# Two layers on one core: an iteration loop written out, row maxima turned by TensorE and sent in two transfers, expert products in new places of the engines' orders

## Chip, core and metric

One core of a Trainium2 chip runs the whole kernel. The metric is the device time of one execution in microseconds (us).

## What is computed

The input x has 2 sequences of 4096 tokens with 512 channels (float32). Two layers follow, cut here to what matters:

```python
# layer 1, "mix": an RWKV recurrence over the tokens, per channel
h = layernorm(x); k = h @ Wk.T; r = h @ Wr.T; v = r
y = wkv_scan(-exp(time_decay), time_first, k, v)   # stable, with a running maximum
x = x + (sigmoid(r) * y) @ Wo.T
# layer 2, "att" and "moe"
h = rmsnorm(layernorm(x)); q = h @ Wq + bq; kv = (h @ Wdown + bdown) @ Wup + bup
att = softmax(q k / sqrt(32))       # over the 16 heads of ONE token, no mixing of tokens
x2 = layernorm(x) + (att @ v) @ Wo + bo
gate = softmax(rmsnorm(x2) @ Wg + bg)             # 8 experts, all of them used
out = x + x2 + sum_e gate_e * (rmsnorm(x2) @ We[e])
```

## The kernel before

The 8192 tokens are cut into 32 tiles of 256. A software pipeline of 34 iterations works on three tiles at once: iteration i does the recurrence ("mix") of tile i, the attention ("att") of tile i-1, the experts ("moe") of tile i-2, and the first norm ("pre") of tile i+1. Each engine walks through its own hand-written list of steps, the same in every iteration (`PE_ORDER`, L132; `DVE_ORDER`, L142; `ACT_ORDER`, L154; `POOL_ORDER`, L164; `SP_ORDER`, L169), and waits on semaphores where it needs another engine's result. An engine never overtakes in its own list, so a step that waits holds up all that stands behind it. `pipeline` (L336) issues the iterations: 0 to 3 written out, 4 to 29 as a hardware loop of 13 passes with two iterations in each (`Fori`, L364), 30 to 33 written out again. In iterations 0 and 1 the expert slots split the weights instead.

Products in float16 have three passes of high and low halves. One expert product, ("moe", u), is one expert for 128 tokens: 12 matmuls of 128x512 into one of two banks (`moe`, L1253); VectorE multiplies it by its gate and adds it to `acc` (`moe`, L1052, the instruction at L1060). There are 16 of them per tile. TensorE may start product u when VectorE is done with u-2.

The attention of one tile, in the order of the data:

- `att_q` (TensorE L1180, ScalarE L630 by way of `heads`, L633) and `att_up` (L1187, L647) make q, k and v. SyncE's `att_up` (L429) copies them by 16 transfers into the stacks `qs` and `ks` (L438 and L442); VectorE's `att_stack` (L975) copies the other rows of `ks`.
- `att_max` (TensorE L1204, the matmuls at L1213): 8 groups of raw scores, "M" 0 to 7, each 4 matmuls into one of a ring of four banks; a group may start when the maximum of the group four before it is done. VectorE takes the maximum of each row (L991) into `mcol` (128 x 32). ("att_max", n) stands for groups 2n and 2n+1.
- `att_m`: VectorE turns `mcol` within squares of 32 (L996) and splits it into two float16 rows (L998, L1000); SyncE sends them into two rows of `qs` with 8 transfers (L445 to L449), so that the next products subtract the maxima by themselves.
- `att_scores` (TensorE L1217, matmuls at L1222; ScalarE's exponential L657) and `att_probs` (TensorE L1226, matmuls at L1232; VectorE divides, L1002): 8 groups each, S0 to S7 and P0 to P7, in the same ring of four banks. P is in float32: for each group 8 recorded matmuls with only 33 columns and 128x128 weights. P k waits for exponential k, and for VectorE's division of P k-2.
- `att_back`, `att_project`, `att_turn2`, `att_gate` end the attention.

In the recurrence, for each half of the channels: VectorE's `mix_decay` (L878), ScalarE's `mix_exp` (L579: four Relu and three exponentials), VectorE's `mix_sum`, `mix_value`, `mix_scan`, `mix_rec` and `mix_gate`, with ScalarE's `mix_num` (L593), and `mix_split` at the end. `mix_project` (TensorE, line names `bank<-w_o,xo`) is the last product that a recurrence tile needs; its start is the mark by which iterations are measured here.

Of the kernel before, what the change touches and what calls it, by code (L numbers as in the profile page):

```python
# [115 lines left out]
ATT_BANK = {use: n % ATT_RING for n, use in enumerate(ATT_USES)}  # L116


def att_before(use):
# [25 lines left out]
    ("mix_value", 0), ("moe", 4), ("att_max", 0), ("att_max", 1), ("att_max", 2), ("att_max", 3), ("att_m", 0),
    ("moe", 5), ("mix_scan", 0), ("moe", 6), ("mix_rec", 0), ("moe", 7), ("mix_rec", 1), ("mix_gate", 0), ("moe", 8),
    ("mix_split", 0), ("att_probs", 0), ("att_probs", 1), ("moe", 9), ("att_probs", 2), ("att_probs", 3),
    ("mix_decay", 1), ("att_probs", 4), ("att_probs", 5), ("moe", 10), ("att_probs", 6), ("att_probs", 7),
    ("att_back", 0), ("mix_sum", 1), ("mix_value", 1), ("moe", 11), ("moe", 12), ("mix_scan", 1), ("att_project", 0),
# [5 lines left out]
    ("mix_turn", 0), ("att_norm", 0), ("moe_gate", 0), ("att_turn", 0), ("mix_k", 0), ("moe", 0), ("moe", 1),  # L155
    ("att_latent", 0), ("att_q", 0), ("att_up", 0), ("mix_v", 0), ("moe", 2), ("moe", 3), ("mix_exp", 0), ("moe", 4),
    ("moe", 5), ("moe", 6), ("moe", 7), ("mix_num", 0), ("att_rest", 0), ("att_scores", 0), ("moe", 8), ("moe", 9),
    ("att_scores", 1), ("mix_split", 0), ("att_scores", 2), ("att_scores", 3), ("att_scores", 4), ("att_scores", 5),
# [15 lines left out]
def build(nc, x, wk, wr, wo1, decay, first, gamma1, wq, bq, wdown, bdown, wup, bup, wo2, bo, gamma2,  # L174
          wg, bg, we, ident_in, kmask_in, qmask_in, out):
    with ExitStack() as ctx:
# [1129 lines left out]
```

## Time and profile before

| | us |
|---|---|
| median of 3 runs | 3222.83 |
| lowest, highest | 3214.9, 3233.78 |
| the profiled execution | 3235.43 |
| its span, first to last instruction | 3233.6 |
| TensorE busy in the span | 2904.1 (90%) |
| VectorE, ScalarE, GpSimd busy | 2221.2 (69%), 1286.2 (40%), 619.2 (19%) |
| mean granted TensorE clock | 0.933 of full speed |

The profile names TensorE PE (PEld: its weight loads), VectorE DVE, ScalarE ACT, GpSimd POOL, SyncE SP; SPq is SyncE's transfer queue. A timeline row has start, length, engine, line, operation, output<-inputs, shapes and a count of merged instructions; in brackets the idle time before it and what ended it. A row of windows has one stretch, its length, the busy time of each engine (with instructions), then the granted clock (1.00 is 2.4 GHz, 0.50 is 1.2 GHz, the only two levels; a value between them is a mix over the stretch), the share of the transfer engines and GB/s.

### The profile page before, as it was taken

The numbers are of one execution on the slowest core, as the hardware profiler recorded it, in microseconds if no ns is written. First come the engines' busy times: TensorE is split into PE (matmuls) and PEld (weight loads), VectorE is DVE, ScalarE is ACT, GpSimd is POOL, SyncE is SP. The second block draws the span as 40 slices with busy tenths as digits, with TensorE's granted clock in tenths as the row PEclk, the third lists the DMA queues.
The fourth block names the chain that finished last, engine by engine and source line by source line (L and its number), as shares of the span: only waits on it lengthen the run. The fifth ranks groups of instructions, "written<-read, shape, count | busy, mean of one in ns | idle before, by whom it ended". The sixth has DMA issues, their size and how long they took to land.

```text
span 3233.6 us, 53881 instructions
## 1 busy us (share of the span) xinstructions
PE 2904.1 (90%) x18864; PEld 1822.3 (56%) x18864; DVE 2221.2 (69%) x4132; ACT 1286.2 (40%) x2399; POOL 619.2 (19%) x681
## 2 busy tenths in 40 slices
PE   2359999999999999999999999999999899999989
PEld 2236665655665655656565565556566565566644
DVE  4787777677666767767676766767766666776663
ACT  2354443433443434444343444444344343444421
POOL 0111122211212212112221121222111221212120
PEclk9669999898999989999998999999899999999999
DMA  6011221101121201121210111220112120212110
GB/s 198 16 18 27 34 34 27 31 24 28 27 34 28 34 21 27 27 34 27 34 31 24 27 27 28 34 34 23 26 27 34 28 33 21 34 21 34 27 20 14
DMA packets 588333, 102.96 MB, mean 32 GB/s; under 512 B 556562, under 2 KB 556690, under 8 KB 588050
## 3 DMA queue, kind: packets, MB, share of 16 engines
q1 hardware_dynamic: 588068, 99.40, 18.0%
q8 instruction: 170, 2.79, 0.4%
q14 instruction: 95, 0.78, 0.1%
HBM read 48.49 MB, written 16.78 MB: 20 GB/s over the span
## 4 chain that ended last, share of the span: by engine, by line
issue 63%; POOL 13%; PE 11%; DVE 7%; SPq 3%; ACT 2%; DMA 1%; POOLq 1%; DVEq 0%; ACTq 0%
PE bank L1080 8%; POOL k L498 2%; POOL x L493 2%; POOL qo L498 2%; POOL acc L520 2%; PE bank L1232 2%; POOL ev L484 2%; POOL zz L480 1%; DVE wkv L895 1%; SPq L442 1%; SPq L438 1%; DVE w_e L827 1%; DVE zz L919 1%; DVE mcol L991 1%; POOL rs L511 1%
## 5 line engine op out<-in xcount | busy, mean ns | idle before, releaser
L1080 PE MATMUL bank<-w_e,h2t 128*128 128x512 f16 x6144 | 1459.4, 396 | 25.8 <-DVE acc L1060 25.8
L1080 PEld LDWEIGHTS bank<-w_e,h2t 128*128 128x128 f16 x6144 | 617.8, 102 | 771.8 <-issue 109.6
L1060 DVE SCALAR_TENSOR_TENSOR acc<-bank,gates,acc 128x512 f32<-128x512 f32 x512 | 370.1, 733 | 173.8 <-PE bank L1080 173.8
L595 ACT ACTIVATE e<-v 128x512 f32<-128x512 f32 x64 | 40.5, 633 | 737.1 <-DVE wkv L895 737.1
L480 POOL TENSOR_TENSOR zz<-wkv,zz 128x512 f32<-128x512 f32 x64 | 105.3, 1645 | 1112.8 <-DVE ev L906 1112.8
L1232 PEld LDWEIGHTS bank<-vp,pr 128*128 128x128 f32 x2048 | 286.6, 214 | 12.8 <-issue 2.4
L1232 PE MATMUL bank<-vp,pr 128*128 128x33 f32 x2048 | 290.8, 292 | 1.9 <-ACT pr L661 1.9
L661 ACT ACTIVATE pr<-bank,col 128x512 f32<-128x512 f32 x256 | 172.5, 686 | 249.1 <-PE bank L1222 249.1
L1080 PE MATMUL bank<-w_o,xo 128*128 128x512 f16 x768 | 176.0, 387 | 78.9 <-DVE xo L857 78.9
L991 DVE TENSOR_REDUCE mcol<-bank 128x4 f32<-128x512 f32 x256 | 158.8, 682 | 114.2 <-PE bank L1213 114.2
L895 DVE TENSOR_TENSOR_SCAN wkv<-e,wkv 128x256 f32<-128x256 f32 x256 | 233.9, 955 | 2.0 <-ACT e L590 2.0
L980 DVE COPY ks<-k 32x1024 f16<-32x1024 f16 x256 | 120.7, 472 | 158.5 <-ACT k L644 151.5
L919 DVE RECIPROCAL zz<-zz 128x256 f32<-128x256 f32 x128 | 223.0, 1743 | 0.0
L498 POOL TENSOR_TENSOR qo<-t,qo 128x256 f16<-128x256 f32 x128 | 87.8, 686 | 467.0 <-ACT qo L644 467.0
L1080 PE MATMUL bank<-w_o,qo 128*128 128x512 f16 x768 | 172.7, 382 | 4.1 <-DVE qo L857 4.1
L1080 PE MATMUL bank<-xo,w_k 128*128 128x256 f16 x1536 | 174.6, 274 | 0.0
L1080 PE MATMUL bank<-ht,w_q 128*128 128x256 f16 x1536 | 173.4, 273 | 0.0
L1080 PE MATMUL bank<-xo,w_r 128*128 128x256 f16 x1536 | 172.9, 273 | 0.0
L1080 PEld LDWEIGHTS bank<-w_o,xo 128*128 128x128 f16 x768 | 73.7, 99 | 173.2 <-DVE xo L857 60.8
L1080 PEld LDWEIGHTS bank<-xo,w_k 128*128 128x128 f16 x1536 | 151.3, 98 | 17.9
L1080 PEld LDWEIGHTS bank<-ht,w_q 128*128 128x128 f16 x1536 | 150.6, 98 | 17.7
L1080 PEld LDWEIGHTS bank<-xo,w_r 128*128 128x128 f16 x1536 | 150.3, 98 | 17.4
(177 smaller groups left out, 3678.7 us busy)
## 6 DMA issues: line engine op xcount, KB each, us to landing
qs<-qo SPq DMA_DIRECT2D x384, 64.0 KB, 3.4
xk<-in_attn_x SPq DMA_DIRECT2D x32, 512.0 KB, 3.6
x<-in_attn_x SPq DMA_DIRECT2D x32, 512.0 KB, 3.6
result<-acc SPq DMA_DIRECT2D x32, 512.0 KB, 2.8
ks<-k SPq DMA_DIRECT2D x128, 64.0 KB, 3.3
w_e<-in_ffn_We SPq DMA_DIRECT2D x7, 1024.0 KB, 13.5
qs<-m SPq DMA_DIRECT2D x256, 2.0 KB, 1.7
qs<-in_attn_Wk SPq DMA_DIRECT2D x1, 1024.0 KB, 5.5
```

Source lines behind the costliest of these rows:

```text
L480: nc.gpsimd.tensor_tensor(zz[:, :, :], wkv[:, 2, :, 0:T], zz[:, :, :], ALU.add).then_inc(mix_pool.sem, 1)
L484: nc.gpsimd.tensor_tensor(ev[:, :, :], wkv[:, 1, :, 0:T], ev[:, :, :], ALU.add).then_inc(mix_pool.sem, 1)
L493: nc.gpsimd.tensor_tensor(x2[:, s, :], x2[:, s, :], bo_row[:, :], ALU.add).then_inc(att_pool.sem, 1)
L498: nc.gpsimd.tensor_tensor(grouped(dst, 1)[:, :, b, :], t32[:, b % 2, :].rearrange("p (g j) -> p g j", g=G), grouped(dst, 0)[:, :, b, :], A ...
L661: nc.scalar.activation(pr[:, k % 2, :], att_bank[ATT_BANK["S", k]][:, :], ACT.Exp, scale=colof["soft"])\
L895: V.tensor_tensor_scan(wkv[:, n, c, 1:T + 1], e1[:, c, :], src[:, c, :], wkv[:, n, c, 0:1], ALU.mult, ALU.add).then_inc(mix_dve.sem, 1)
L919: V.reciprocal(zz[:, c, :], zz[:, c, :]).then_inc(mix_dve.sem, 1)
L980: V.tensor_copy(ks[n * HD:(n + 1) * HD, :, f, :], grouped(k16, 0)[f * HD:(f + 1) * HD].rearrange("p g b j -> p g (b j)")).then_inc(att_dve ...
L991: V.tensor_reduce(mcol[:, 4 * k:4 * k + 4], att_bank[ATT_BANK["M", k]][:, :].rearrange("p (g x) -> p g x", g=4), AX, ALU.max).then_inc(att ...
L1060: V.scalar_tensor_tensor(out=acc[:, s, :], in0=moe_bank[u % 2][:, :], scalar=gates[:, s, e:e + 1], in1=acc[:, s, :], op0=ALU.mult, op1=ALU ...
L1080: ins = nc.tensor.matmul(dst, left(a), right(b), start=(n == 0), stop=(n == last))
L1232: ins = nc.tensor.matmul(att_bank[ATT_BANK["PV", k]][:, n * (HD + 1):(n + 1) * (HD + 1)], pr[:, k % 2, n * P:(n + 1) * P], vp[:, 4 * k + n ...
```

## The change

- `pipeline` issues all 34 iterations written out; the hardware loop is gone.
- Row maxima: TensorE turns `mcol` (new step ("att_m", 0) of `PE_ORDER`, a transposition 128x32 into 32 partitions x 128 of the bank of M7), VectorE splits it from there (two instructions in place of three), and SyncE sends each of the two rows with one transfer, 2 in place of 8. The ring's wait for the bank of M7 is moved to the split.
- New orders for TensorE, VectorE and ScalarE. On TensorE, among the steps around the attention: expert product 2 goes ahead of `att_up`; 3, 4 and 5 stand before the maxima, which are then in one piece; 6, the turn, 7 and 8 follow; 9 stays after S0 and S1; 10 and 11 go in among the score and value products, 12 and 13 between them and `att_project`. On VectorE, 0 and 1 go ahead of `att_latent` and 2 ahead of `mix_decay`; `att_vt` is ahead of 3; the second half's `mix_decay`, `mix_sum` and `mix_value` go in among the divisions. On ScalarE, the second `mix_exp` goes between exponentials 4 and 5, and `mix_num` 0 behind exponential 1.

```diff
 PE_ORDER = [
     ("mix_turn", 0), ("moe", 0), ("moe", 1), ("att_turn", 0), ("mix_k", 0), ("att_latent", 0), ("att_q", 0),
-    ("att_up", 0), ("mix_v", 0), ("moe", 2), ("moe", 3), ("moe", 4), ("att_max", 0), ("att_max", 1), ("moe", 5),
-    ("att_max", 2), ("att_max", 3), ("moe", 6), ("moe", 7), ("moe", 8), ("att_scores", 0), ("att_scores", 1),
-    ("moe", 9), ("att_probs", 0), ("att_scores", 2), ("att_probs", 1), ("att_scores", 3), ("att_probs", 2),
-    ("att_scores", 4), ("att_probs", 3), ("att_scores", 5), ("att_probs", 4), ("att_scores", 6), ("att_probs", 5),
-    ("att_scores", 7), ("moe", 10), ("att_probs", 6), ("att_probs", 7), ("moe", 11), ("moe", 12), ("att_project", 0),
-    ("moe", 13), ("moe", 14), ("moe", 15), ("att_turn2", 0), ("mix_project", 0), ("att_gate", 0),
+    ("moe", 2), ("att_up", 0), ("mix_v", 0), ("moe", 3), ("moe", 4), ("moe", 5), ("att_max", 0), ("att_max", 1),
+    ("att_max", 2), ("att_max", 3), ("moe", 6), ("att_m", 0), ("moe", 7), ("moe", 8), ("att_scores", 0),
+    ("att_scores", 1), ("moe", 9), ("att_probs", 0), ("att_scores", 2), ("att_probs", 1), ("att_scores", 3),
+    ("att_probs", 2), ("att_scores", 4), ("moe", 10), ("att_probs", 3), ("att_scores", 5), ("att_probs", 4),
+    ("moe", 11), ("att_scores", 6), ("att_probs", 5), ("att_scores", 7), ("att_probs", 6), ("att_probs", 7),
+    ("moe", 12), ("moe", 13), ("att_project", 0), ("moe", 14), ("moe", 15), ("att_turn2", 0), ("mix_project", 0),
+    ("att_gate", 0),
 ]
 DVE_ORDER = [
...
+    ("att_stats", 0), ("att_norm", 0), ("mix_turn", 0), ("moe_gate", 0), ("att_turn", 0), ("moe", 0), ("moe", 1),
+    ("att_latent", 0), ("moe", 2), ("mix_decay", 0), ("att_stack", 0), ("att_vt", 0), ("moe", 3), ("mix_sum", 0),
+    ("moe", 4), ("mix_value", 0), ("att_max", 0), ("att_max", 1), ("att_max", 2), ("att_max", 3), ("moe", 5),
+    ("att_m", 0), ("moe", 6), ("mix_scan", 0), ("mix_rec", 0), ("moe", 7), ("mix_rec", 1), ("mix_gate", 0),
+    ("moe", 8), ("att_probs", 0), ("mix_split", 0), ("att_probs", 1), ("mix_decay", 1), ("att_probs", 2), ("moe", 9),
+    ("att_probs", 3), ("att_probs", 4), ("mix_sum", 1), ("mix_value", 1), ("moe", 10), ("att_probs", 5), ("moe", 11),
+    ("att_probs", 6), ("att_probs", 7), ("att_back", 0), ("mix_scan", 1), ("mix_rec", 2), ("moe", 12), ("moe", 13),
+    ("att_project", 0), ("mix_rec", 3), ("mix_gate", 1), ("moe", 14), ("mix_split", 1), ("pre_stats", 0), ("moe", 15),
...
 ACT_ORDER = [
...
+    ("moe", 5), ("moe", 6), ("moe", 7), ("att_rest", 0), ("att_scores", 0), ("att_scores", 1), ("moe", 8),
+    ("mix_num", 0), ("mix_split", 0), ("moe", 9), ("att_scores", 2), ("att_scores", 3), ("att_scores", 4),
+    ("mix_exp", 1), ("att_scores", 5), ("moe", 10), ("att_scores", 6), ("att_scores", 7), ("moe", 11),
...
-        m_in = Steps(sem("m_in"), 16, m=2 * F)
+        m_in = Steps(sem("m_in"), 16, m=2)
...
-                    "M": (att_dve, "smax", k), "S": (att_act, "ex", k), "PV": (att_dve, "norm", 2 * k + 1),
+                    "M": (att_dve, "m_lo", 0) if k == 7 else (att_dve, "smax", k), "S": (att_act, "ex", k), "PV": (att_dve, "norm", 2 * k + 1),
...
-            for i in range(4):
-                iteration(i, i % 2, i // 2)
-            with eng.Fori(0, (NT - 6) // 2) as pair:
-                for par in range(2):
-                    iteration(pair * 2 + (4 + par), par, pair + 2)
-            for i in range(NT - 2, NT + 2):
+            for i in range(NT + 2):
                 iteration(i, i % 2, i // 2)
...
-                    for f in range(F):
-                        sp.dma_start(qs[SCAN_ROWS + l:SCAN_ROWS + l + 1, :, f, :], m16[f * G:(f + 1) * G, l, :]).then_inc(m_in.sem, 16)
+                    sp.dma_start(qs[SCAN_ROWS + l:SCAN_ROWS + l + 1, :, :, :].rearrange("a g f x -> a g (f x)"), m16[:, l, :]).then_inc(m_in.sem, 16)
...
-                dve.wait_ge(*att_dve.done(t, "smax"))
-                V.transpose(mturn[:, :], mcol[:, :]).then_inc(att_dve.sem, 1)
-                dve.wait_ge(*att_dve.done(t, "m_turn"))
-                V.tensor_scalar(m16[:, 0, :], mturn[:, :], -2.0 ** -14, None, ALU.mult).then_inc(att_dve.sem, 1)
+                turned_m = att_bank[TURNED_M][0:G, 0:P]
+                dve.wait_ge(*att_pe.done(t, "MT0"))
+                V.tensor_scalar(m16[:, 0, :], turned_m, -2.0 ** -14, None, ALU.mult).then_inc(att_dve.sem, 1)
...
+            def att_m(t, _):
+                pe.wait_ge(*att_dve.done(t, "smax"))
+                nc.tensor.transpose(att_bank[TURNED_M][0:G, 0:P], mcol[:, :], ident[:, :]).then_inc(att_pe.sem, 1)
```

## Rows read from the trace of the kernel before

**Rows 1.** The page, part 1: busy time, share of the span, instructions.

```profile
PE 2904.1 (90%) x18864; PEld 1822.3 (56%) x18864; DVE 2221.2 (69%) x4132; ACT 1286.2 (40%) x2399; POOL 619.2 (19%) x681
```

**Rows 2.** Timeline of TensorE: `mix_project` in iterations 2, 5, 29 and 31.

```profile
325.75 5.35 PE L1080 MATMUL bank<-w_o,xo 128*128 128x512 f16 x24 [0.55 <-DVE xo L857]
...
601.27 5.35 PE L1080 MATMUL bank<-w_o,xo 128*128 128x512 f16 x24 [0.75 <-DVE xo L857]
...
2908.68 5.35 PE L1080 MATMUL bank<-w_o,xo 128*128 128x512 f16 x24 [0.77 <-DVE xo L857]
...
3093.95 5.35 PE L1080 MATMUL bank<-w_o,xo 128*128 128x512 f16 x24 [0.55 <-DVE xo L857]
```

**Rows 3.** TensorE's waits from 601.27 to 2908.68: total us, times, longest.

```profile
PE bank L1213 <- DMA ks<-k: 65.0, 24, 3.1
PE bank L1110 <- issue: 39.4, 12, 3.6
PE bank L1080 <- DVE xo L857: 19.0, 25, 0.8
PE bank L1080 <- DVE acc L1060: 16.0, 24, 0.7
PE bank L1196 <- ACT t L641: 7.9, 24, 0.3
```

**Rows 4.** Windows: whole iterations and the loop's 24 iterations, with the granted clock.

```profile
325.75:415.25 89.50, 85.23 (x588) 53.78 (x589) 66.41 (x125) 39.04 (x74) 19.25 (x21) 1.00 0.19 30
601.27:2908.68 2307.41, 2160.80 (x14113) 1355.31 (x14113) 1600.38 (x2977) 936.41 (x1753) 460.62 (x504) 0.95 0.18 29
1281.53:1371.18 89.65, 85.21 (x589) 53.76 (x589) 66.59 (x125) 38.97 (x74) 19.20 (x21) 1.00 0.19 31
```

**Rows 5.** Windows: S0 to `att_project`, at full clock and in its slowest case.

```profile
1337.40:1356.43 19.03, 19.03 (x145) 13.53 (x145) 14.83 (x34) 10.70 (x18) 0.00 (x0) 1.00 0.09 28
1715.36:1739.40 24.04, 24.04 (x145) 16.50 (x144) 14.98 (x33) 10.70 (x18) 0.00 (x0) 0.79 0.07 23
```

**Rows 6.** Windows of one iteration: start to M0 (with pass change), M0 to S0.

```profile
1947.23:1996.03 48.80, 42.39 (x296) 28.63 (x297) 25.90 (x56) 21.35 (x43) 11.62 (x14) 0.93 0.32 45
1996.03:2010.69 14.66, 13.99 (x80) 7.31 (x81) 11.56 (x19) 2.04 (x3) 1.09 (x1) 0.89 0.01 1
```

**Rows 7.** Timeline of TensorE in the iteration from 1281.53.

```profile
1324.26 1.06 PE L1213 MATMUL bank<-ks,qs 104*128 104x128 f16 x16 [2.68 <-DMA ks<-k]
...
1337.41 0.62 PE L1222 MATMUL bank<-qs,ks 106*128 106x128 f16 x8
...
1340.46 0.97 PE L1232 MATMUL bank<-vp,pr 128*128 128x33 f32 x8
...
1346.96 2.75 PE L1080 MATMUL bank<-w_e,h2t 128*128 128x512 f16 x12
1349.55 1.87 PE L1232 MATMUL bank<-vp,pr 128*128 128x33 f32 x16
```

**Rows 8.** Timeline of SyncE's queue in the same iteration.

```profile
1308.37 5.67 SPq L438 DMA_DIRECT2D qs<-qo  x8
...
1318.76 2.75 SPq L442 DMA_DIRECT2D ks<-k  x4
1331.15 5.00 SPq L449 DMA_DIRECT2D qs<-m  x8
```

**Rows 9.** Timelines of VectorE and, last two, of ScalarE in the same iteration.

```profile
1324.69 2.48 DVE L991 TENSOR_REDUCE mcol<-bank 128x4 f32<-128x512 f32 x4 [1.77 <-PE bank L1213]
...
1345.17 0.15 DVE L879 COPY wkv<-carry 128x6 f32<-128x6 f32 x1
...
1348.75 0.91 ACT L586 ACTIVATE e<-e,wcol 128x256 f32<-128x256 f32 x2
...
1350.60 0.61 ACT L591 ACTIVATE zz<-zz 128x512 f32<-128x512 f32 x1
```

**Rows 10.** Line L1110, the float32 turns on TensorE: shortest, median, longest ns.

```profile
L1110 PE MATMUL bank<-ident,hrow x512: 272/273/473, 141.2 to 3183.7; 128*128 128x128 f32 x171
```

More of the change, by code:

```diff
@@ L116 @@
 ATT_BANK = {use: n % ATT_RING for n, use in enumerate(ATT_USES)}
+TURNED_M = ATT_BANK["M", 7]
 def att_before(use):
@@ L140 @@
+    ("att_probs", 2), ("att_scores", 4), ("moe", 10), ("att_probs", 3), ("att_scores", 5), ("att_probs", 4),
+    ("moe", 11), ("att_scores", 6), ("att_probs", 5), ("att_scores", 7), ("att_probs", 6), ("att_probs", 7),
+    ("moe", 12), ("moe", 13), ("att_project", 0), ("moe", 14), ("moe", 15), ("att_turn2", 0), ("mix_project", 0),
+    ("att_gate", 0),
 ]
 DVE_ORDER = [
-    ("att_stats", 0), ("att_norm", 0), ("mix_turn", 0), ("moe_gate", 0), ("att_turn", 0), ("att_latent", 0),
-    ("mix_decay", 0), ("moe", 0), ("moe", 1), ("att_stack", 0), ("moe", 2), ("att_vt", 0), ("moe", 3), ("mix_sum", 0),
@@ L145 @@
[L145 to L149, printed above, removed]
@@ L150 @@
-    ("mix_rec", 2), ("moe", 13), ("mix_rec", 3), ("mix_gate", 1), ("moe", 14), ("mix_split", 1), ("pre_stats", 0),
-    ("moe", 15), ("pre_norm", 0), ("att_turn2", 0), ("mix_project", 0),
+    ("att_stats", 0), ("att_norm", 0), ("mix_turn", 0), ("moe_gate", 0), ("att_turn", 0), ("moe", 0), ("moe", 1),
+    ("att_latent", 0), ("moe", 2), ("mix_decay", 0), ("att_stack", 0), ("att_vt", 0), ("moe", 3), ("mix_sum", 0),
+    ("moe", 4), ("mix_value", 0), ("att_max", 0), ("att_max", 1), ("att_max", 2), ("att_max", 3), ("moe", 5),
@@ L152 @@
+    ("pre_norm", 0), ("att_turn2", 0), ("mix_project", 0),
 ]
 ACT_ORDER = [
[L155 to L158, printed above, removed]
@@ L159 @@
-    ("att_scores", 6), ("att_scores", 7), ("moe", 10), ("mix_exp", 1), ("att_back", 0), ("moe", 11), ("moe", 12),
-    ("mix_num", 1), ("moe", 13), ("att_square", 0), ("att_norm2", 0), ("moe", 14), ("moe", 15), ("mix_split", 1),
-    ("att_turn2", 0), ("pre_norm", 0),
+    ("mix_turn", 0), ("att_norm", 0), ("moe_gate", 0), ("moe", 0), ("att_turn", 0), ("moe", 1), ("mix_k", 0),
+    ("moe", 2), ("moe", 3), ("att_latent", 0), ("att_q", 0), ("att_up", 0), ("mix_v", 0), ("mix_exp", 0), ("moe", 4),
@@ new lines @@
+    ("moe", 5), ("moe", 6), ("moe", 7), ("att_rest", 0), ("att_scores", 0), ("att_scores", 1), ("moe", 8),
+    ("mix_num", 0), ("mix_split", 0), ("moe", 9), ("att_scores", 2), ("att_scores", 3), ("att_scores", 4),
+    ("mix_exp", 1), ("att_scores", 5), ("moe", 10), ("att_scores", 6), ("att_scores", 7), ("moe", 11),
+    ("att_back", 0), ("moe", 12), ("moe", 13), ("moe", 14), ("moe", 15), ("att_square", 0), ("mix_num", 1),
+    ("att_norm2", 0), ("mix_split", 1), ("att_turn2", 0), ("pre_norm", 0),
@@ L240, in build @@
         pr = sb("pr", [P, 2, 4 * P])
-        mcol, mturn, m16 = sb("mcol", [P, G]), sb("mturn", [P, CB * NJ]), sb("m16", [P, 2, CB * NJ], F16)
+        mcol, m16 = sb("mcol", [P, G]), sb("m16", [G, 2, P], F16)
         rden = sb("rden", [P, G])
@@ L311, in build @@
         mix_pool = Steps(sem("mix_pool"), **{f"{s}_{h}": c for h in (0, 1) for s, c in wkv_pool})
-        att_pe = Steps(sem("att_pe"), **{f"{n}{k}": 1 for n, k in ATT_USES})
+        att_pe = Steps(sem("att_pe"), **{step: 1 for n, k in ATT_USES for step in ([f"{n}{k}"] + ["MT0"] * (f"{n}{k}" == "M7"))})
         att_act = Steps(sem("att_act"), h=2, h_hi=2, c=2, q=8, k=8, v=4, xn=2, ex=8, ot_hi=2, sq=2,
@@ L315, in build @@
         att_dve = Steps(sem("att_dve"), stats=2, idle=1, aggr=2, var=2, shift=2, h_lo=2, c_lo=1, stack=8,
-                        vt=1, smax=8, m_turn=1, m_hi=1, m_lo=1, norm=16, ot=1, ot_lo=2, x2=2, h2_lo=2)
+                        vt=1, smax=8, m_hi=1, m_lo=1, norm=16, ot=1, ot_lo=2, x2=2, h2_lo=2)
         gate_dve = Steps(sem("gate_dve"), gl=1, gmax=1, gsub=1, gsum=1, grec=1, gmul=1, gates=1)
@@ L994, in att_m @@
             def att_m(t, _):
-                dve.wait_ge(*att_dve.done(t, "smax"))
-                V.transpose(mturn[:, :], mcol[:, :]).then_inc(att_dve.sem, 1)
-                dve.wait_ge(*att_dve.done(t, "m_turn"))
-                V.tensor_scalar(m16[:, 0, :], mturn[:, :], -2.0 ** -14, None, ALU.mult).then_inc(att_dve.sem, 1)
+                turned_m = att_bank[TURNED_M][0:G, 0:P]
+                dve.wait_ge(*att_pe.done(t, "MT0"))
+                V.tensor_scalar(m16[:, 0, :], turned_m, -2.0 ** -14, None, ALU.mult).then_inc(att_dve.sem, 1)
                 dve.wait_ge(*att_dve.done(t, "m_hi"))
-                lo(m16[:, 1, :], mturn[:, :], -2.0 ** -14, m16[:, 0, :]).then_inc(att_dve.sem, 1)
+                lo(m16[:, 1, :], turned_m, -2.0 ** -14, m16[:, 0, :]).then_inc(att_dve.sem, 1)
             def att_probs(t, k):
@@ L1262, in _ @@
             pipeline(pe, PE_ORDER, {"mix_turn": mix_turn, "mix_k": mix_k, "mix_v": mix_v, "mix_project": mix_project,
-                          "att_turn": att_turn, "att_latent": att_latent, "att_q": att_q, "att_up": att_up, "att_max": att_max, "att_scores": att_scores, "att_probs": att_probs,
+                          "att_turn": att_turn, "att_latent": att_latent, "att_q": att_q, "att_up": att_up, "att_max": att_max, "att_m": att_m, "att_scores": att_scores, "att_probs": att_probs,
                           "att_project": att_project, "att_turn2": att_turn2,
```

## The prediction

> **What bounds the kernel now.** I read the page first: TensorE is busy for 90% of the span, no other engine for more than 69% [rows 1], so the time is TensorE's work, its idle gaps and its clock. Next, its timeline. The starts of `mix_project` give the length of an iteration. From iteration 5 to 29 there are 24 inside the hardware loop: (2908.68 - 601.27) / 24 = 96.14 us [rows 2]. They take 2307 of 3233.6 us, so the iteration decides. The windows show how long one can be: 89.65 us at a granted clock of 1.00, in the loop as in the written-out part (89.50) [rows 4]. So 96.14 is made of three things.
>
> - The loop's own gap. 12 times in those 24 iterations TensorE stood still for "issue", 39.4 us in all, once for each new pass [rows 3]: 1.64 us per iteration. The iteration of 89.65 has none.
> - Clock. 96.14 - 89.65 - 1.64 = 4.85 us. The loop's mean clock of 0.95 says the same: 0.05 x 96.14 = 4.8 [rows 4].
> - Waits that the 89.65 still holds, per iteration: 2.7 for the stack `ks` ahead of M0, 0.67 for VectorE's `acc` ahead of expert product 7, 0.76 ahead of `mix_project`, 0.33 in `att_up` [rows 3], 4.5 together.
>
> Where does the clock fall? Behind two kinds of stretch. In the first, TensorE is idle: the 3.3 us at a new pass (that part at 0.93) and the 2.7 us ahead of M0 (0.89 from there to S0, which costs 0.11 x 14.7 = 1.6 us) [rows 6]. In the second it is "busy" all the time: S0 to `att_project` takes 19.0 us at 1.00, but 24.0 at 0.79 in the worst case [rows 5]; there the float32 products of 33 columns run for 1346.96 - 1340.46 = 6.5 us with no expert product between them [rows 7]. Over the 24 iterations this second stretch lost time in 22 and 2.4 us on average, from 0 to 5.0, about half of the 4.85; the rest goes about equally to the pass change (1.35) and the wait ahead of M0 (1.1).
>
> The Trainium skill (TensorE: Matmul & The Clock Gate, "HAM oscillation") puts the fall of the clock down to waits between bursts. By that rule alone the second stretch, which has no idle time, would lose nothing, and the new places of the products would give nothing there. The trace disagrees at 0.79.
>
> **The change, part by part,** per iteration, against the 96.14.
>
> 1. Loop written out: the gap goes, -1.64, and the low clock behind it, -1.35. Nothing takes the gap's place: the written-out iterations of before hold the same instructions and reach 89.50 [rows 4]. Bounds: -3.0 to 0 (if the gap is not the loop's). I take all. The Trainium skill (Runtime: NRT & Kernel Launch, "Instruction fetch mechanics") says that code is fetched straight ahead and a taken branch stalls on it; this trace agrees, with 39.4 us at 12 branches.
>
> 2. Expert product 2 ahead of `att_up`. Behind `att_q`, TensorE now has four products ahead of M0 (2, and 3 to 5) where it had three (2 to 4), so it reaches M0 one product later: 2.59 us (1346.96 to 1349.55 [rows 7]). The transfers to `ks` hang on SyncE's queue, which starts with q at 1308.37 and is solid to 1321.5 [rows 8]; q is not moved, and k, 1.1 us later, is still ready before its turn comes. So M0 starts when it did and the wait shrinks from 2.7 to some 0.5: -2.2. The 0.33 wait in `att_up` goes too: its bank has had 2.6 us more. What may be late next is VectorE: it now waits in its list for product 2 before `mix_decay`, which holds up `att_stack`, the sum and `mix_value` ahead of the maxima. I find it free 1.4 us before M0.
>
> 3. Maxima in one piece. 8 groups in a ring of four: M7 waits for maximum 3, at 0.62 us each (2.48 / 4 [rows 9]). Until now an expert product lay between, and the groups took 2 x 0.9 us; now about 3.2: +1.4 (bounds 0 and 2.5, eight full maxima less the groups). Product 6 covers the last four maxima.
>
> 4. The turn. A float32 turn on TensorE is 0.27 us [rows 10], and with the hand-over from the last maximum I take +0.4 (0.3 to 1.0). It waits for all maxima; behind it in the list are products 7 and 8 and the scores. VectorE does product 5 first, so 7 finds its bank free: the 0.67 goes. VectorE saves one instruction of 0.2 us: nothing, no one waits for it. The 8 transfers took 5.0 us to issue [rows 8]; 2 take about 1.2. Products 7 and 8 (5.2 us) cover issue and landing, as three products covered the 8 before. So the fewer transfers give 0 to -0.4; I take 0.
>
> 5. Scores and values. The 6.5 us without a dense product become stretches of about 3.3, 2.0 and 3.0 us (three, two and three groups of 1.09, less an S). The trace has a stretch of 1.9 us (two groups, after 1349.55 [rows 7]) with no fall behind it, and the 6.5 with nearly always one. 3.3 is nearer to 1.9: I take 0.6 of the 2.4 us as left, -1.8 (0 to -2.4). Ahead of M0 the wait is 0.5 in place of 2.7, but the ring makes short gaps: 0.3 left of 1.1, -0.8 (0 to -1.1).
>
> 6. The recurrence's second half starts earlier, so its last step is ready when TensorE asks: -0.76 (0 to -0.76). `att_back` still has two products (12, 13) of cover.
>
> Sum at full clock: 89.65 - 2.2 - 0.33 + 1.4 + 0.4 - 0.67 - 0.76 = 87.5. With 0.9 of clock: 88.4, that is 7.7 less than 96.14. Over the loop's 24: -186. The five written-out iterations of before (2 to 4, 29, 30) take 275.5 + 185.3 = 460.8 [rows 2]; at 88.4 each, -19. Iterations 0, 1 and the last three: 0 (+-10), they wait for weights and VectorE. 3233.6 - 205 = 3029, and 1.8 around the span: about 3030. The profiled execution (3235.4) lies 12.6 above the median of the three; I leave the forecast unshifted, since low clock, part of that scatter, is what is taken away.
>
> **Rivals.** A. *The score stretch stays cold*: 3.3 us of 33-column products is still enough for a fall. For it: 22 of 24. +1.8 x 29 = +52: 3085. B. *VectorE late ahead of the maxima* (part 2's slack is 1.4 us and rests on hand-overs of 0.1): 1.5 us per iteration, +43: 3075. C. *All of it lands*: no loss of clock, gaps of 87.1 us: -1.3 x 29, 2990. D. *The gap isn't the loop's* and shows up in written-out code too, with its clock: +3.0 x 24 = +72: 3100. Against it: [rows 4], 89.50. E. *Slower*: ScalarE's second `mix_exp` stands between exponentials 4 and 5 and waits for `mix_decay`, at most 3.6 us (1345.17 to 1348.75), behind division 1; then 2.5 us of its own (to 1351.21) [rows 9] and 0.7 for exponential 5. P5 needs that, and in the new order starts 13 us after S0; I make it ready at 12 to 12.5. Each us beyond is 1 us per iteration, and behind P5 stand all of VectorE's divisions. It makes the kernel slower than the median of before only from (3223 - 3030) / 29 = 6.7 us beyond that slack; 8 us beyond give 3262. No row shows such a delay.
>
> **How the numbers follow.** Forecast 0.60 (its own range 3005 to 3060), A 0.14, B 0.09, C 0.08, D 0.04, E 0.03, else 0.02. A range of 2985 to 3095 holds the first four and takes in the bounds of parts 3 to 6. A measurement of this kernel tells 0.5% (16 us) from no change; only E and the unnamed rest reach that far: faster 0.95, same 0.02, slower 0.03.
>
> **What would show it.** Right: no "issue" wait of 3 us on TensorE; `mix_project` starts about 88 us apart; the wait ahead of M0 at 0.5; M0 to S0 about 11.5 us in place of 13.1; mean clock above 0.97 in mid-span; 10 and 11 warm among the score products. A: the starts 90 apart and the clock near 0.9 between S0 and P7. B: a wait for `ks` gone but the maxima late. E: TensorE waits for ScalarE at L1232. Wrong altogether: iterations above 93 us.

## The result, and the profile after

The changed kernel takes **2969.99 us** (median of 4 runs, 2969.81 to 2976.66), the kernel before 3228.31 beside it (4 runs, the three shown among them). The ratio is **0.9208**, 95% interval 0.9171 to 0.9246 (ratios here are worked out from the single runs and differ a little from the quotient of the medians). The forecast was 3030 with a range of 2985 to 3095: the sign and the places were right, and the measured time lies 15 us under the range.

The profiled execution took 2970.13 us, its span is 2968.3. The page's first lines and its row of granted clocks, in 40 slices of the span:

```profile
span 2968.3 us, 47758 instructions
PE 2786.5 (94%) x18896; PEld 1761.5 (59%) x18896; DVE 2170.1 (73%) x4100; ACT 1294.7 (44%) x2399; POOL 610.0 (21%) x681
PEclk9569999999999999999999999999999999999999
```

TensorE is busy for 94% of the span in place of 90% [rows 1], and yet its busy time fell by 118 us, with 32 more instructions (the turns). That is the clock: the same matmuls ran longer before, while an iteration at full clock has nearly the same busy time in both (85.21 [rows 4], and 85.44 below). The row of clocks is nines from the fourth slice to the last.

The iteration is again read from the starts of `mix_project`, iteration 5 and iteration 29:

```profile
573.04 5.34 PE L1075 MATMUL bank<-w_o,xo 128*128 128x512 f16 x24
...
2657.53 5.34 PE L1075 MATMUL bank<-w_o,xo 128*128 128x512 f16 x24
```

(2657.53 - 573.04) / 24 = **86.85 us**, against 96.14 before [rows 2] and 88.4 forecast. The bracket with the wait for `xo` is gone from both rows. Here are TensorE's waits over the same 24 iterations (total, times, longest), all that there are:

```profile
PE bank L1208 <- DVE mcol L987: 14.4, 72, 0.2
PE bank L1208 <- DMA ks<-k: 5.6, 11, 0.9
```

Beside [rows 3]: "issue" 39.4, `xo` 19.0, `acc` 16.0 and `t` 7.9 are all gone, the wait for `ks` fell from 65.0 to 5.6, and one new wait has come, 3 times 0.2 per iteration, for the ring between the maxima. Windows of the 24 iterations, of one of them, and of its stretch from S0 to `att_project` (length, then busy time of PE, PEld, DVE, ACT, POOL; granted clock; DMA share; GB/s), and below them two disturbed stretches, M0 to S0 of iteration 22 and S0 to `att_project` of iteration 23:

```profile
573.04:2657.53 2084.49, 2061.33 (x14138) 1303.42 (x14136) 1561.63 (x2953) 943.56 (x1753) 454.59 (x504) 1.00 0.19 31
1610.80:1696.96 86.16, 85.44 (x591) 54.24 (x589) 65.05 (x124) 39.31 (x74) 18.92 (x21) 1.00 0.19 32
1663.96:1685.73 21.77, 21.77 (x157) 14.78 (x156) 18.67 (x39) 11.22 (x19) 4.10 (x3) 1.00 0.07 25
...
2085.95:2098.71 12.76, 12.04 (x69) 6.01 (x70) 10.44 (x18) 0.00 (x0) 1.08 (x1) 0.87 0.01 1
2185.08:2208.53 23.45, 23.45 (x157) 15.23 (x156) 20.21 (x41) 11.22 (x19) 5.19 (x4) 0.93 0.09 23
```

Read (1 - clock) x length as what the clock costs. It costs something in only 5 of the 24 iterations: 22 and 28 from M0 to S0 (1.7 us each, behind the two longest waits for `ks`, 0.92 and 0.90 us), 23, 24 and 26 from S0 to `att_project` (1.64 each). That is 8.3 us in 24 iterations, 0.35 per iteration, where 4.85 had been lost and 0.9 was forecast. (The stretch from S0 is longer than the 19.03 of [rows 5] because it now holds five expert products, not four.)

Where the 265.3 us of span went (3233.6 - 2968.3):

| stretch | before | after | gain | forecast |
|---|---|---|---|---|
| 24 iterations, 5 to 28 | 2307.4 | 2084.5 | 222.9 | 186 |
| iterations 2 to 4, 29, 30 | 460.8 | 433.4 | 27.4 | 19 |
| iteration 1 | 95.6 | 87.1 | 8.5 | 0 |
| iteration 0, head and tail | 369.8 | 363.3 | 6.5 | 0 |

The new order in its own timeline, TensorE in the iteration from 1610.80:

```profile
1635.41 2.75 PE L1075 MATMUL bank<-w_e,h2t 128*128 128x512 f16 x12
...
1644.99 7.93 PE L1075 MATMUL bank<-w_e,h2t 128*128 128x512 f16 x36
1652.76 1.57 PE L1208 MATMUL bank<-ks,qs 104*128 104x128 f16 x20
1654.53 0.40 PE L1208 MATMUL bank<-ks,qs 104*128 104x128 f16 x4 [0.20 <-DVE mcol L987]
...
1655.96 2.75 PE L1075 MATMUL bank<-w_e,h2t 128*128 128x512 f16 x12
1658.55 0.27 PE L1214 MATMUL bank<-ident,mcol 128*32 128x128 f32 x1
1658.77 5.35 PE L1075 MATMUL bank<-w_e,h2t 128*128 128x512 f16 x24
1663.96 0.61 PE L1221 MATMUL bank<-qs,ks 106*128 106x128 f16 x8
```

Product 2, then 3 to 5 (x36), then the eight maxima in 3.20 us with three short waits, product 6, the turn in 0.22 us from start to start, products 7 and 8, and S0. M0 to S0 is 11.20 us; 11.5 was forecast. The DMA issues of the same iteration, SyncE's queue:

```profile
1637.55 5.81 SPq L435 DMA_DIRECT2D qs<-qo  x8
1643.41 3.25 SPq L439 DMA_DIRECT2D qs<-qo  x4
1646.71 2.82 SPq L439 DMA_DIRECT2D ks<-k  x4
1659.17 1.20 SPq L445 DMA_DIRECT2D qs<-m  x2
```

The last of the `ks` issues ends at 1649.53, 3.2 us ahead of M0. In [rows 8] that was 1321.51, 2.8 us ahead of an M0 that had waited for them for 2.7 [rows 7]. The two transfers of the maxima take 1.20 us to issue in place of 5.00.

### The profile page after: what moved, and what is told of

Read it like the earlier page. It is cut to its first block, busy times and chain, and to the rows that moved or that the text cites. A ratio compares the mean times of both kernels' runs of the same rounds, so it can differ in the third digit from the quotient of the medians.

```text
span 2968.3 us, 47758 instructions
## 1 busy us (share of the span) xinstructions
PE 2786.5 (94%) x18896; PEld 1761.5 (59%) x18896; DVE 2170.1 (73%) x4100; ACT 1294.7 (44%) x2399; POOL 610.0 (21%) x681
## 4 chain that ended last, share of the span: by engine, by line
PE 83%; DVE 6%; SPq 5%; DMA 2%; ACT 2%; issue 1%; POOL 0%; ACTq 0%; DVEq 0%
PE bank L1075 69%; PE bank L1231 8%; PE bank L1105 3%; SPq L439 3%; DVE mcol L987 3%; PE bank L1221 2%; DMA ks<-k 2%; SPq L435 2%; PE bank L1191 1%; ACT t L637 1%; PE bank L1208 1%; DVE mx L725 1%; DVE zz L915 0%; DVE w_e L823 0%; SPq L392 0%
## 5 line engine op out<-in xcount | busy, mean ns | idle before, releaser
L1075 PE MATMUL bank<-w_e,h2t 128*128 128x512 f16 x6144 | 1390.8, 382 | 5.3 <-DVE acc L1055 5.3
L1075 PEld LDWEIGHTS bank<-w_e,h2t 128*128 128x128 f16 x6144 | 598.8, 99 | 686.5 <-issue 17.5
L1231 PE MATMUL bank<-vp,pr 128*128 128x33 f32 x2048 | 267.9, 276 | 5.1 <-ACT pr L657 5.0
L1231 PEld LDWEIGHTS bank<-vp,pr 128*128 128x128 f32 x2048 | 260.1, 196 | 17.3 <-DVE rden L1000 3.6
L891 DVE TENSOR_TENSOR_SCAN wkv<-e,wkv 128x256 f32<-128x256 f32 x256 | 177.1, 732 | 3.2 <-ACT e L586 3.2
L480 POOL TENSOR_TENSOR ev<-wkv,ev 128x512 f32<-128x512 f32 x64 | 69.7, 1089 | 422.1 <-DVE wkv L891 422.1
L669 ACT ACTIVATE hrow<-x 128x512 f32<-128x512 f32 x64 | 40.3, 629 | 232.0 <-DVE x L1017 232.0
```

Of the source, the lines that this page charges most:

```text
L480: nc.gpsimd.tensor_tensor(ev[:, :, :], wkv[:, 1, :, 0:T], ev[:, :, :], ALU.add).then_inc(mix_pool.sem, 1)
L891: V.tensor_tensor_scan(wkv[:, n, c, 1:T + 1], e1[:, c, :], src[:, c, :], wkv[:, n, c, 0:1], ALU.mult, ALU.add).then_inc(mix_dve.sem, 1)
L1075: ins = nc.tensor.matmul(dst, left(a), right(b), start=(n == 0), stop=(n == last))
L1231: ins = nc.tensor.matmul(att_bank[ATT_BANK["PV", k]][:, n * (HD + 1):(n + 1) * (HD + 1)], pr[:, k % 2, n * P:(n + 1) * P], vp[:, 4 * k + n ...
```

## The experiments

Ten kernels ran. Each ratio is against the kernel before on the same chip (its medians there: 3231.04 for the first four runs below, 3227.62 for the next four, 3218.41 for the last two). "Above the change" is the median less 2969.99; since the kernel before scatters by 13 us between those groups, a difference below that decides nothing, and the iteration mean, again from iteration 5 to 29, is given beside it.

| run | median us | ratio | above the change | iteration us |
|---|---|---|---|---|
| unroll_only | 3149.02 | 0.9764 [0.9699, 0.9830] | 179 | 92.84 |
| loop_kept | 3048.55 | 0.9462 [0.9398, 0.9527] | 79 | 89.71 |
| old_scores | 3056.68 | 0.9493 [0.9424, 0.9561] | 87 | 89.46 |
| old_maxima | 3028.40 | 0.9384 [0.9315, 0.9452] | 58 | 89.04 |
| five_behind | 3085.80 | 0.9556 [0.9515, 0.9598] | 116 | 90.83 |
| new_scores_alone | 3067.72 | 0.9506 [0.9461, 0.9552] | 98 | 90.13 |
| two_behind_up | 2976.46 | 0.9219 [0.9178, 0.9260] | 6 | 87.06 |
| maxima_split | 2988.77 | 0.9263 [0.9217, 0.9309] | 19 | 87.59 |
| eight_transfers | 3022.34 | 0.9386 [0.9340, 0.9433] | 52 | 88.63 |
| maxima_split2 | 2976.29 | 0.9234 [0.9193, 0.9275] | 6 | 87.37 |

**unroll_only.** The kernel before with its loop written out, nothing else.

```
-            for i in range(4):
-                iteration(i, i % 2, i // 2)
-            with eng.Fori(0, (NT - 6) // 2) as pair:
...
+            for i in range(NT + 2):
                 iteration(i, i % 2, i // 2)
```

> The kernel before with nothing but the loop written out. Theory (the 3.3 us stop at each of 12 passes is the loop's, and the low clock right behind it comes from that stop): 39 us of stops and some 34 us of clock go, 3160 us (3140 to 3185); the falls of the clock between S0 and att_project and ahead of M0 stay, mean iteration about 93.1 us. Rival (the stop is code loading that any code of this length meets, so it only moves to another place): 3220 to 3235, with 'issue' waits of about 3 us still on TensorE.

Measured 3149.02. TensorE's waits over its 24 iterations:

```profile
PE bank L1208 <- DMA ks<-k: 53.4, 24, 3.0
PE bank L1075 <- DVE acc L1055: 16.0, 24, 0.7
PE bank L1075 <- DVE xo L852: 13.7, 24, 0.9
PE bank L1217 <- DMA qs<-m: 6.2, 8, 1.1
PE bank L1191 <- ACT t L636: 6.0, 24, 0.3
```

"Issue" is gone, and no stop stands in its place (the new wait for `m` is 6.2 / 24 = 0.26 us): rival D falls. The iteration fell by 3.30 us, 3.0 forecast; 1.64 of it is the gap. From `mix_project` to M0, the part with the pass change, low clock had cost 32.5 us in the 24 iterations and now costs 1.4. Elsewhere it still costs time, 0.04 x 92.84 = 3.7 us per iteration in all:

```profile
606.43:2834.68 2228.25, 2132.71 (x14112) 1338.22 (x14113) 1595.47 (x2977) 938.90 (x1753) 463.16 (x504) 0.96 0.18 29
```

**loop_kept.** The other way round: the changed kernel with the loop of before.

```
-            for i in range(NT + 2):
+            for i in range(4):
+                iteration(i, i % 2, i // 2)
+            with eng.Fori(0, (NT - 6) // 2) as pair:
...
```

> The kernel after with the hardware loop of before put back. Theory: 12 stops of 3.3 us (39 us) and the clock behind them, at most 34 us: 3010 to 3045 us. If the clock behind the stop is only low because of other stretches of the old orders, the stops alone: 3010. Rival (in the new orders something else covers the stop): 2970 to 2980.

Measured 3048.55, a little over what was expected. The largest wait is back, 12 times:

```profile
PE bank L1110 <- issue: 40.6, 12, 3.7
PE bank L1213 <- DMA ks<-k: 13.2, 23, 1.2
```

One of the twelve on TensorE's timeline, and the window of the 9 us behind it:

```profile
1115.16 0.75 PE L1080 MATMUL bank<-w_g,h2t 128*128 128x8 f16 x24
1119.36 1.97 PE L1110 MATMUL bank<-ident,xk 128*128 128x128 f32 x8 [3.44 <-issue]
```

```profile
1120.20:1129.20 9.00, 9.00 (x40) 4.75 (x39) 3.66 (x11) 3.33 (x6) 3.46 (x3) 0.74 0.19 58
```

The turns of `xk` take 1.97 us where the changed kernel takes 1.07, and the clock is 0.74: the engine goes on at 1.2 GHz behind its stop. In 9 of the 12 pass changes the clock cost 1.7 or 3.4 us more, 22 us in all, in 3 nothing. So a pass costs 3.4 us of standing and on average 1.8 of clock: 63 of the 69 us that separate the two kernels' 24 iterations. Most of the rest is the wait for `ks`, 13.2 us in place of 5.6. The Trainium skill (Runtime: NRT & Kernel Launch, "Instruction fetch mechanics") says that a taken branch outside the fetched stretch stalls the engine while straight code is fetched ahead; both runs agree, with 12 stalls where the loop is and none where it isn't. That the stop is spent on fetching no row shows; the runs show only that it belongs to the loop.

**old_scores.** The changed kernel with the three lists as before from the scores on: 10 behind S7, none between P2 and S7.

```
-    ("att_probs", 2), ("att_scores", 4), ("moe", 10), ("att_probs", 3), ("att_scores", 5), ("att_probs", 4),
-    ("moe", 11), ("att_scores", 6), ("att_probs", 5), ("att_scores", 7), ("att_probs", 6), ("att_probs", 7),
...
+    ("att_probs", 2), ("att_scores", 4), ("att_probs", 3), ("att_scores", 5), ("att_probs", 4), ("att_scores", 6),
+    ("att_probs", 5), ("att_scores", 7), ("moe", 10), ("att_probs", 6), ("att_probs", 7), ("moe", 11), ("moe", 12),
...
```

> The kernel after, with the three lists from the first scores on as before (expert product 10 ahead of P6, 11 and 12 behind P7, second mix_decay, mix_sum, mix_value and mix_exp late). Theory (33-column products without dense ones between them make the clock fall, idle or not): granted clock near 0.87 between S0 and att_project in most iterations, +2.4 us of clock and +0.8 us of the wait ahead of mix_project per iteration, 3050 to 3070 us. Rival (only idle time makes the clock fall): clock 1.00 there, only the wait comes back, about 2995 us.

Measured 3056.68. From S0 to `att_project` it lost clock in 18 of 24 iterations, 45.1 us, 1.9 per iteration; M0 to S0 lost in 7, 11.7 us. `mix_project` waits again:

```profile
PE bank L1074 <- DVE xo L852: 13.3, 24, 0.6
```

Clock 2.0 more than in the changed kernel plus 0.6 of wait is the whole 2.6 by which the iteration is longer. Now iteration 7, in which TensorE did not wait for `ks`: first M0 to S0, which is at full clock, then S0 to `att_project`:

```profile
811.45:822.66 11.21, 10.49 (x71) 5.32 (x70) 10.57 (x18) 2.04 (x3) 1.84 (x2) 1.00 0.01 3
822.66:843.35 20.69, 20.69 (x146) 14.10 (x145) 15.58 (x34) 10.70 (x18) 0.00 (x0) 0.92 0.08 27
```

PE is busy for all of the 20.69 us, and at full clock these matmuls took 19.03 [rows 5]. The timeline shows where the clock falls, at S7 and product 10, behind 6.3 us of scores and float32 products from P0 (825.70) on:

```profile
832.00 0.61 PE L1220 MATMUL bank<-qs,ks 106*128 106x128 f16 x4
832.41 4.21 PE L1074 MATMUL bank<-w_e,h2t 128*128 128x512 f16 x12
```

At full clock they take 0.39 and 2.75 us. In 11 of the 18 iterations it is like this, with the stretch ahead at full clock; in the other 7 it had lost some too. So the clock fell with no idle time, in a stretch of float32 products of 33 columns, and no longer falls there, but for 3 iterations in 24, when expert products break that stretch up. The Trainium skill (TensorE: Matmul & The Clock Gate, "HAM oscillation") names waits between bursts as the cause of such falls. By that rule alone old_scores would have lost only its 0.6 us of wait; the run decides against it as the only cause. The run puts back VectorE's and ScalarE's lists too, but TensorE waits for neither between S0 and `att_project`, here as in the change, so what differs for it there is its own order. What it is in the stretch that lets the clock fall, the 33 columns, the float32, the weight loads or the scores of 128 columns between them, no run separates.

**old_maxima and eight_transfers.** Does sending the maxima in two transfers matter? old_maxima puts back VectorE's turn and the 8 transfers; eight_transfers keeps TensorE's turn and only sends in 8 pieces:

```
-                    sp.dma_start(qs[SCAN_ROWS + l:SCAN_ROWS + l + 1, :, :, :].rearrange("a g f x -> a g (f x)"), m16[:, l, :]).then_inc(m_in.sem, 16)
+                    for f in range(F):
+                        sp.dma_start(qs[SCAN_ROWS + l:SCAN_ROWS + l + 1, :, f, :], m16[:, l, f * G:(f + 1) * G]).then_inc(m_in.sem, 16)
...
```

> The kernel after, with the maxima turned by VectorE and sent in 8 transfers, as before (no turn on TensorE). Theory now: VectorE splits them only after expert product 5, the 8 transfers take 5.0 us to issue and 1.7 to land, so they come some 1.5 us after products 7 and 8 are done: S0 waits 1.5 to 2 us in each of 31 iterations, 3010 to 3035 us, with some clock lost. Rival, as the prediction had it (8 transfers are covered by products 7 and 8, 2 transfers bring nothing): 2960 to 2972 us.

> The kernel after with TensorE's turn kept, but the maxima sent in 8 transfers. Theory (the number of transfers is what made S0 wait in old_maxima; each takes SyncE 0.6 us to issue): S0 waits 1.0 to 1.7 us per iteration, 3010 to 3035 us, as old_maxima. Rival (VectorE's own turn and its later split made S0 wait): 2968 to 2980 us.

Measured 3028.40 and 3022.34: nearly all of old_maxima's 58 us is in the number of transfers; what who turns adds, 6 us, is within the scatter. Of eight_transfers, the largest wait, SyncE's queue, and TensorE at S0:

```profile
PE bank L1222 <- DMA qs<-m: 32.1, 24, 2.2
```

```profile
1692.68 5.00 SPq L446 DMA_DIRECT2D qs<-m  x8
```

```profile
1698.88 0.62 PE L1222 MATMUL bank<-qs,ks 106*128 106x128 f16 x8 [1.23 <-DMA qs<-m]
```

The issues alone run to 1697.68, and S0 waits 1.23 us: it starts 6.20 us behind the first issue, where TensorE was ready after 4.97. In the kernel before, the first issue had been at 1331.15 and S0 at 1337.41, 6.26 us later [rows 7, 8]. What covered the 8 transfers there was products 7 and 8, the wait of 0.66 ahead of 7 and only the last 0.1 us of 6, just enough; the new order takes that wait away. 32.1 / 24 = 1.34 us per iteration is the wait for `m`; the iteration is longer by 1.78, and 0.2 of the rest is clock.

**five_behind.** Three products ahead of M0 instead of four; the rest as in the change.

```
-    ("moe", 2), ("att_up", 0), ("mix_v", 0), ("moe", 3), ("moe", 4), ("moe", 5), ("att_max", 0), ("att_max", 1),
-    ("att_max", 2), ("att_max", 3), ("moe", 6), ("att_m", 0), ("moe", 7), ("moe", 8), ("att_scores", 0),
+    ("moe", 2), ("att_up", 0), ("mix_v", 0), ("moe", 3), ("moe", 4), ("att_max", 0), ("att_max", 1),
+    ("att_max", 2), ("att_max", 3), ("moe", 5), ("moe", 6), ("att_m", 0), ("moe", 7), ("moe", 8), ("att_scores", 0),
```

> The kernel after, with expert product 5 on TensorE behind the maxima instead of ahead of them, so that M0 is reached 2.59 us earlier. Theory (M0 starts when SyncE's queue has sent ks, and only the number of products ahead of it decides what of that is waited for): the wait for ks comes back at 2.4 to 2.9 us in each of 31 iterations, with about 1 us of clock in half of them: 3045 to 3085 us. Rival (the transfers come early enough anyway in the new orders): under 0.5 us of wait, 2965 to 2985 us.

Measured 3085.80, just over the upper edge. The wait is 64.0 / 24 = 2.67 us per iteration, as in the kernel before [rows 3]. The loss of clock had been expected far too small: from M0 to S0 it cost 1.7 or 3.4 us in every iteration, 2.6 on average, as much as the wait itself:

```profile
PE bank L1208 <- DMA ks<-k: 64.0, 24, 3.6
```

```profile
1177.23:1193.43 16.20, 16.00 (x81) 7.67 (x82) 10.53 (x18) 0.00 (x0) 2.06 (x2) 0.79 0.01 2
```

The kernel before, with the same wait, lost clock there in only 14 of its 24 iterations, 1.3 us on average. Its maxima stand in two pieces with a product between, here all eight follow the wait in one piece; that this is the reason was not tried by itself.

**two_behind_up.** Product 2 back behind `att_up` and `mix_v`, so still four ahead of M0 (VectorE takes it behind `att_stack`).

```
-    ("moe", 2), ("att_up", 0), ("mix_v", 0), ("moe", 3), ("moe", 4), ("moe", 5), ("att_max", 0), ("att_max", 1),
+    ("att_up", 0), ("mix_v", 0), ("moe", 2), ("moe", 3), ("moe", 4), ("moe", 5), ("att_max", 0), ("att_max", 1),
...
```

> The kernel after, with expert product 2 behind mix_v instead of ahead of att_up (VectorE takes it behind att_stack). The number of products ahead of M0 stays the same. Theory (only that number matters for the wait ahead of M0): the same but for the gap of 0.3 to 0.5 us in att_up, 2970 to 2990 us. Rival (the place ahead of att_up is what removes the wait, by giving q's or k's transfers another time): a wait of over 1 us for ks is back, 3000 us or more.

Measured 2976.46, not to be told from the change. The wait in `att_up` is back and that for `ks` gone almost wholly:

```profile
PE bank L1191 <- ACT t L637: 6.1, 24, 0.3
PE bank L1208 <- DMA ks<-k: 1.0, 2, 0.7
```

What counts is the number of products between the transfers and M0, not which side of `att_up` they lie on.

**new_scores_alone.** The changed kernel with its lists up to product 8 as before, but for the turn (TensorE does it between 6 and 7); the new score lists stay.

```
-    ("moe", 2), ("att_up", 0), ("mix_v", 0), ("moe", 3), ("moe", 4), ("moe", 5), ("att_max", 0), ("att_max", 1),
+    ("att_up", 0), ("mix_v", 0), ("moe", 2), ("moe", 3), ("moe", 4), ("att_max", 0), ("att_max", 1), ("moe", 5),
...
```

> The kernel after (written out, turn by TensorE, 2 transfers), with the three lists up to expert product 8 as before; the part from the scores on is new. Theory (the parts add up): the waits ahead of M0, in att_up and at product 7 are back, about 3 us of gaps and 1.1 us of clock per iteration less the ring's 1.4: 91 us per iteration, 3060 to 3100 us, with no clock lost from S0 to att_project except right behind a fall of before. Rival (the new part from the scores on is what matters, the wait ahead of M0 is taken up by work that is late anyway): 2985 to 3020 us.

Measured 3067.72. The waits are those of before, that for `acc` doubled:

```profile
PE bank L1208 <- DMA ks<-k: 52.5, 24, 2.8
PE bank L1075 <- DVE acc L1055: 32.3, 24, 1.3
PE bank L1191 <- ACT t L637: 6.0, 24, 0.3
```

The score stretch, with the new lists, lost clock in 7 of the 24 iterations, and in each of the 7 the stretch ahead of it had lost some already. Both windows of iteration 9, M0 to S0 and S0 to `att_project`:

```profile
988.30:1003.77 15.47, 14.12 (x81) 6.90 (x82) 11.39 (x18) 0.00 (x0) 1.09 (x1) 0.89 0.01 2
1003.77:1027.23 23.46, 23.46 (x158) 15.20 (x156) 19.60 (x41) 11.22 (x19) 5.20 (x4) 0.93 0.07 24
```

M0 to S0 lost clock in 10 iterations: in 7 of them the score stretch lost some as well, and in none of the other 14. One fall is often followed by the next.

The prices of the four parts, each undone by itself (79 loop, 87 scores, 98 order up to product 8, 58 turn and transfers), add up to 322 us, more than the 258 that the change brings. The 58 is nearly the surplus: the kernel before had no wait for `m` [rows 3], so fewer transfers would have brought little in its order, and without them the three others add up to 264.

**maxima_split and maxima_split2.** Can the ring's +1.4 be had back? Product 6 goes between maxima 1 and 2 on TensorE, 7 ahead of the turn. In the first, VectorE does product 5 between its maxima and 6 behind the turned row; in the second, 6 ahead of it too:

```
-    ("att_max", 2), ("att_max", 3), ("moe", 6), ("att_m", 0), ("moe", 7), ("moe", 8), ("att_scores", 0),
+    ("moe", 6), ("att_max", 2), ("att_max", 3), ("moe", 7), ("att_m", 0), ("moe", 8), ("att_scores", 0),
```

> The kernel after, with expert product 6 between the second and third pair of maxima (VectorE does product 5 there), 7 between the maxima and the turn, 8 behind it. Theory: the ring's waits go (1.4 us), but the two transfers have only product 8 over them, so S0 waits 0.6 to 1.0 us: 0.4 to 0.8 us per iteration faster than after, 2945 to 2960 us. Rival (the wait for the maxima's transfers is over 1.4 us, or the clock falls more often): 2970 to 3000 us.

> As maxima_split, but VectorE adds product 6 ahead of the split of the maxima. Theory (in maxima_split, products 8 and 9 on TensorE waited for VectorE's sums of 6 and 7, held up behind the split: 1.3 and 0.5 us; the ring's waits did go): those waits fall under 0.6 us in all, M0 to S0 takes 10.2 to 10.6 us in place of 11.2, VectorE's divisions come some 0.5 us late: 2950 to 2965 us. Rival (what the ring's waits give is lost to VectorE in any order, since it is behind from here to P2): 2968 to 2990 us.

Measured 2988.77 and 2976.29 (6 runs, 2959.03 to 2981.99), neither faster than the change; both theories missed, and both times lie in the rival's range. The largest wait of the first:

```profile
PE bank L1075 <- DVE acc L1055: 44.6, 48, 1.3
```

and of the second, with the place where it shows on TensorE's timeline:

```profile
PE bank L1075 <- DVE acc L1055: 20.6, 23, 1.0
PE bank L1221 <- DMA qs<-m: 8.1, 24, 2.0
```

```profile
1586.74 2.76 PE L1075 MATMUL bank<-w_e,h2t 128*128 128x512 f16 x12 [0.95 <-DVE acc L1055]
```

In the second, M0 to S0 is 10.1 us, 1.1 less than in the change, and S0 to `att_project` is 1.1 longer: product 9 waits for product 7's bank, which VectorE reads late. What the first version of the two saves between the maxima, and the second between M0 and S0, comes back as a wait for `acc` behind it. An iteration of maxima_split2 without a fall takes 86.2 us, as in the change; its mean is higher because the clock fell in 11 of its 24 score stretches, 18.8 us in all. No order tried here has less than the change's 86.85.

## Why the prediction was right in kind and too high

What bounds the kernel, and the parts at which time would go, held: no "issue" wait, starts of `mix_project` below 90 us apart, M0 to S0 at 11.2, clock 1.00 in mid-span. Of the cases, it was rival C (0.08) that came in, all of it landing, and a little more than C had: 86.85 against its 87.1. A fell (3 score stretches in 24 lose time), B fell, D fell by unroll_only, E did not come. By the steps:

1. *Loop, -1.64 and -1.35.* Right: 3.30 in unroll_only, and 89.71 - 86.85 = 2.86 in loop_kept.

2. *Part 2, -2.2 and -0.33.* Right in kind, mis-sized. From start to start, the stretch from `mix_v` to M0 without its products is 2.85 us shorter in a full-clock iteration, and `att_up` 0.50 (2.25 to 1.75). The wait that is left averages 5.6 / 24 = 0.23, where I put 0.5. "So M0 starts when it did" is not quite so: in iterations without a pass change the last issue for `ks` had ended 39.7 to 40.1 us behind `mix_project`, and now it ends after 38.7 to 40.1. TensorE reaches M0 at 42.0 and waits in 11 of the 24. VectorE's slack, which rival B doubted, is enough, but smaller than the "free 1.4 us before M0" of the prediction: its last task ahead of the maxima ends at 1652.40, 0.36 us before M0 and 0.80 us before the first maximum is due, on its own timeline:

```profile
1651.71 0.69 DVE L904 TENSOR_TENSOR e<-e,v 128x512 f32<-128x512 f32 x1
1653.19 4.87 DVE L987 TENSOR_REDUCE mcol<-bank 128x4 f32<-128x512 f32 x8 [0.80 <-PE bank L1208]
```

3. *Ring, +1.4.* Right: 3.20 us for the eight groups, less 2 x 0.9.

4. *Turn +0.4, product 7 -0.67, transfers 0.* The turn is 0.22. Product 7's wait gave 0.83. "The fewer transfers give 0 to -0.4" holds only for the sum: before and after there is no wait for `m`. But "as three products covered the 8 before" misreads the rows: two products, a wait and 0.1 us of the third covered them (see eight_transfers), and in the new order two products don't cover eight. Without the two transfers the new order would cost 52 us. That edit has its price in what it allows.

5. *Clock, 0.6 of 2.4 and 0.3 of 1.1 left.* The trace of before has 21 score stretches that lost time, not 22, and at 2.6 us on average. Right in kind: 4.9 us in 24 iterations are left in the score stretch (0.20 each), 3.4 ahead of S0 (0.14). Together 0.35, not 0.9, so 0.55 x 24 = 13 us of the error.

6. *Recurrence, -0.76.* From `att_project` to `mix_project` without products it is 0.93 less.

**The step that failed** is the sum at full clock. It was "87.5"; measured is 86.85 - 0.35 = 86.5. Behind it stood "waits that the 89.65 still holds ... 4.5 together", each gap taken from the idle time that a row shows in brackets. But the end that the profile gives to a run of matmuls lies past the start of the next: in the timeline above, product 6 "ends" at 1655.96 + 2.75 = 1658.71, and the turn behind it has started at 1658.55. So 0.16 us of a gap is hidden under the matmul ahead of it. From starts alone the four gaps gave 2.85 + 0.50 + 0.83 + 0.93 = 5.1 us where the brackets had 2.68 + 0.33 + 0.67 + 0.76 = 4.4. The forecast took 2.2 + 0.33 + 0.67 + 0.76 = 4.0 of them, since it left 0.5 of the first; less the 0.23 that is left of it on average, 4.9 came. That is 0.9 of the 1.0 us: four times 0.17 from the brackets, and 0.27 from the wait for `ks`. (The turn's 0.18 less and 0.15 more in the score stretch cancel.) Over 24 iterations 1.0 is 24 us, the largest single part of the 60 us by which the forecast was too high; the clock is 13, the five written-out iterations 8 and the ends 15.

**The second failure** is "iterations 0, 1 and the last three: 0 (+-10)". Iteration 1 has the same lists and lost 7.3 us of clock before and 1.0 after: it gained 8.5, and iteration 0, head and tail 6.5 more. Both errors and the clock point the same way, which the range did not allow for: its lower end stood 5 us under rival C, whose price came from the same idle columns.

E's slack, the one that a worse order would have eaten, is small. ScalarE's exponential 5 is done 12.0 us after S0 (1675.32 + 0.67), and P5 starts 13.6 us after it (1677.54): 1.5 us.

```profile
1675.32 0.67 ACT L657 ACTIVATE pr<-bank,col 128x512 f32<-128x512 f32 x1
```

## What to carry to other kernels

When TensorE is nearly always busy, look at its granted clock by stretch before looking for gaps, and at stretches of narrow float32 products as well as at waits: a dense product of a neighbouring task put among them cost nothing here and saved 2 us per iteration. Price gaps from the starts of the instructions around them, not from the idle time in brackets, and price each gap's clock with it: in five_behind a wait of 2.7 us was followed by 1.7 or 3.4 us lost to low clock. An edit that gains nothing in the sum (two transfers for eight) can still be what another edit stands on, so ask of each what the new order would cost without it.

## What the runs showed of the hardware that was not expected

- The clock falls with TensorE busy throughout, in 18 of 24 iterations of old_scores, each at a cost of 1.7 or 3.4 us.
- Twelve passes of a loop cost 40.6 us of standing still in loop_kept, and 22 us lost to low clock behind it, in 9 of the 12.
- The time to issue the same four transfers of `qs<-qo` (L439) on SyncE varies from 2.9 to 4.8 us between iterations of the changed kernel, with one issue of up to 2.6 us among others of 0.6 to 0.7. In the kernel before it was 4.1 to 4.6. Its cause is open; nothing was tried on it.
